# Routing sixteen tiles in groups of 4, 4, 4, 2 and 2

## What is computed

```python
x = x + L0_xattn(ctx_768, layernorm(x), mask)
x = x + L0_ffn(layernorm(x))
x = x + L1_xattn(layernorm(x), ctx_768)      # 8 heads, 77 keys
x = x + L1_ffn(layernorm(x))
...
def L1_ffn(x, router_w, w1, b1, w2, b2):
    capacity = max(1, int(Sz * 2.0 / E) + 1)                 # 257 of 1024
    scores = softmax(einsum('bsd,ed->bse', x, router_w))
    gate_vals, sel_idx = top_k(swapaxes(scores, 1, 2), capacity)
    tokens = x[b_idx, sel_idx]
    h = gelu(einsum('becd,edh->bech', tokens, w1) + b1)
    y = einsum('bech,ehd->becd', h, w2) + b2
    return zeros_like(x).at[b_idx, sel_idx].add(y * gate_vals[..., None])
```

## Time and profile before

| what | us |
|---|---|
| median of 3 runs | 962.7 (961.96 to 964.91) |
| the profiled execution | 963.34 |
| its span in the trace | 961.6 |
| mean granted clock of TensorE over the span | 0.919 of full |
| TensorE busy | 804.0 (84%) |
| VectorE, ScalarE, GpSimd busy | 552.2, 401.0, 354.6 |

### The profile page before, as it was taken

The page is one execution under the profiler, slowest core; times in us unless marked ns, Lnnn a source line. Parts: engine busy times, 40 slices in busy tenths (PEclk is TensorE's granted clock), DMA queues, the critical chain, the costliest instruction groups (busy, mean ns, idle before and its releaser), DMA issues.

```text
span 961.6 us, 12810 instructions
## 1 busy us (share of the span) xinstructions
PE 804.0 (84%) x4832; PEld 639.9 (67%) x4832; DVE 552.2 (57%) x1132; ACT 401.0 (42%) x719; POOL 354.6 (37%) x302
## 2 busy tenths in 40 slices
PE   2649988989999999988999786885139999899998
PEld 2536554755655555767789676875029988898897
DVE  5766686566666673454434477763846355655532
ACT  2324543454444334541532343332116555565563
POOL 6523112210220112243431343321443587657863
PEclk9959999999999999997999698896559999999999
DMA  6000000000000100100020201111210453245422
GB/s 174 1 0 1 1 1 1 1 1 1 1 1 0 45 3 1 44 1 3 1 84 1 88 1 45 45 45 49 93 45 6 133 138 102 47 127 137 131 30 23
DMA packets 21371, 39.70 MB, mean 41 GB/s; under 512 B 4489, under 2 KB 16893, under 8 KB 19005
## 3 DMA queue, kind: packets, MB, share of 16 engines
q1 hardware_dynamic: 14653, 30.44, 9.4%
q0 software_dynamic: 6656, 8.43, 5.0%
HBM read 30.32 MB, written 8.40 MB: 40 GB/s over the span
## 4 chain that ended last, share of the span: by engine, by line
PE 48%; DVE 20%; POOL 14%; issue 11%; ACT 5%; DMA 1%; SPq 0%; ACTq 0%; POOLq 0%; DVEq 0%
PE ps L410 14%; PE ps L549 9%; PE ps L649 5%; POOL out_dram L2351 4%; DVE mx L1152 4%; PE ps L989 4%; POOL gt L2222 3%; PE ps L513 3%; POOL wh L2346 3%; PE ps L566 2%; PE ps L567 2%; DVE qkn L1111 2%; PE ps L490 2%; POOL wh L2343 1%; DVE rep L1526 1%
## 5 line engine op out<-in xcount | busy, mean ns | idle before, releaser
L549 PE MATMUL ps<-PT,VA 128*65 128x512 f32 (+1 forms) x288 | 147.5, 594 | 0.2 <-ACT PT L1760 0.2
L989 PE MATMUL ps<-wh,he 128*128 128x256 f32 (+1 forms) x960 | 127.5, 289 | 0.0
L989 PEld LDWEIGHTS ps<-wh,he 128*128 128x128 f32 (+1 forms) x960 | 112.2, 171 | 6.7
L1760 ACT ACTIVATE PT<-ps 128x512 f32<-128x512 f32 x128 | 76.0, 594 | 67.5 <-PE ps L567 67.0
L1152 DVE TENSOR_REDUCE mx<-ps 128x1 f32<-128x1104 f32 x64 | 83.5, 1305 | 34.2 <-PE ps L513 34.0
L410 PE MATMUL ps<-GT,wh 128*128 128x258 f32 x768 | 95.5, 285 | 2.7 <-ACT het L2018 1.5
L410 PEld LDWEIGHTS ps<-GT,wh 128*128 128x128 f32 x768 | 94.2, 191 | 3.7 <-ACT het L2018 1.9
L2081 POOL TENSOR_TENSOR ssq<-ssq,half 128x4 f32<-128x4 f32 x32 | 32.4, 1013 | 127.3 <-DVE ssq L1093 127.0
L1628 DVE TENSOR_TENSOR he<-het,he 128x516 fp32r<-128x516 f32 x64 | 44.9, 702 | 59.0 <-ACT he L1654 52.5
L2072 POOL TENSOR_TENSOR rs<-rs,half 128x4 f32<-128x4 f32 (+1 forms) x18 | 17.4, 969 | 162.3 <-DVE rs L1025 162.1
L2351 POOL DMA_INDIRECT out_dram<-ye,idx x40 | 66.1, 1654 | 23.1 <-ACT ye L1654 16.0
(11 more groups left out here) (251 smaller groups left out, 1591.1 us busy)
## 6 DMA issues: line engine op xcount, KB each, us to landing
wr<-in_w1e_dram SPq DMA_DIRECT2D x8, 1024.0 KB
wr<-in_w2e_dram SPq DMA_DIRECT2D x8, 1024.0 KB
x<-in_x_dram SPq DMA_DIRECT2D x4, 512.0 KB, 7.6
w<-in_w_dram SPq DMA_DIRECT2D x2, 1024.0 KB, 4.7
y_dram<-yr SPq DMA_DIRECT2D x4, 512.0 KB, 3.0
out_dram<-x SPq DMA_DIRECT2D x4, 512.0 KB, 4.2
b2e<-in_b2e_dram SPq DMA_DIRECT2D x8, 128.0 KB
gt<-y_dram,idx POOLq DMA_INDIRECT x40
```

Source lines behind the costliest of these rows:

```text
L549: pe.matmul(bank[6 + hf][0:65, :], VA[b][0:K, kt, h, :], PT[u % 4][0:K, :], start=kt == 0, stop=kt == 8).then_inc(p_pv, 1)
L989: op = pe.matmul(bank[bk][0:M, 0:256], he[j][:, m, c0:c0 + M], w2h[i][:, 256 * m:256 * m + 256], start=n == 0, stop=n == 23)
L1760: a.activation(PT[u % 4][0:K, :], bank[4 + u % 2][0:K, :], ACT.Exp, bias=0.0 if K == 128 else mcol[:, b:b + 1]).then_inc(a_exp, 1)
```

## The change

`ROUTE` divides the router's work into five groups: tiles 0 to 3, 4 to 7, 8 to 11, 12 and 13, 14 and 15. `router` is split in two: `route_norm(r)` goes up to the normalised tiles, `route_pick(r)` takes them from the transposes to rep and scT. The statistics of a tile are now taken in `product` directly behind its addition to x, held by its semaphore. The last two groups have buffers of their own (yr2, xf2) and banks of their own (4 and 5 for the transposes, 7 and 6 for the logits). In `route_pick` they copy both halves of a tile pair in one ScalarE instruction.

```diff
+ROUTE = [(0, 4), (4, 4), (8, 4), (12, 2), (14, 2)]
...
+def last_routes(p2, n4, p3, p4):
+
+    drain(n4)
+    for stream in (p2, p2, p3, p4, p3, p3, p4, p4, p2, p3, p3, p4, p4):
+        next(stream, None)
+    drain(p2, p3, p4)
...
                 v.tensor_tensor(x[:, n, :], bank[1 + n % 2][:, 0:256], x[:, n, :], ALU.add).then_inc(v_x1, 1)
+                v.wait_ge(v_x1, n + 1)
+                step(v.bn_stats(stats[:, n, :], x[:, n, :]))
...
-            def router(g, banks, delay=0, gap=0):
-                yield from idle(delay)
-                v.wait_ge(v_x1, 4 * g + 4)
-                yield from norm(("r", g), lambda i: x[:, 4 * g + i, :], 4 * g, 4)
-                means(4 * g, ("r", g))
...
+            def route_norm(r):
+                t0, n = ROUTE[r]
+                settle()
+                for i in range(n):
+                    op = v.bn_aggr(mv[:, t0 + i, :], stats[:, t0 + i, :])
+                step(op)
+                settle()
+                v.tensor_scalar(rs[:, t0:t0 + n], mv[:, t0:t0 + n, 1], 1.0, 1e-5, ALU.mult, ALU.add).then_inc(v_var, 1)
+                yield
+                v.wait_ge(g_rstd, NORM["r", r])
+                v.scalar_tensor_tensor(nmr[:, t0:t0 + n], mv[:, t0:t0 + n, 0], -1.0, rs[:, t0:t0 + n],
+                                       ALU.mult, ALU.mult).then_inc(v_nmr, 1)
...
+                for i in range(1, n, 2):
+                    op = centred(normed_tile(r, i), x[:, t0 + i, :], t0 + i)
...
-            for g in range(1, 4):
-                qs = queries(g + 1, q_) if g < 3 else idle(0)
+            for g in range(1, 3):
+                qs = queries(g + 1, q_)
                 ns_ = norm_n(3) if g == 1 else idle(0)
-                rs_ = router(g - 1, (0,), 4, 1)
+                rs_ = both(idle(6 if g == 1 else 3), route_norm(g - 1), idle(1 if g == 1 else 4), route_pick(g - 1, 0))
                 merge(attention1(g), (qs, 0.6), (ns_, 0.8), (rs_, 1.0))
                 drain(qs, ns_, rs_)
-            drain(router(3, (0, 3)))
+            rs_ = both(idle(3), route_norm(2), idle(8), route_pick(2, 0))
+            merge(attention1(3), (rs_, 1.0), (both(idle(12), route_norm(3)), 1.0))
+            last_routes(rs_, route_norm(4), route_pick(3, 7), route_pick(4, 6))
...
-            v.wait_ge(a_scT, 2)
-            v.wait_ge(p_repT, 2)
-            v.wait_ge(d_out, 64)
+            v.wait_ge(a_scT, 3)
+            v.wait_ge(p_repT, 3)
...
+            def route_pick(r, turn, rb):
+                t0, n = ROUTE[r]
...
+                    a.wait_ge(p_rT, turns(r))
+                    copy(xf2[:, :, 256 * (r - 3):256 * (r - 3) + 256],
+                         bank[turn[0]].rearrange("p (k n) -> p k n", k=2)).then_inc(a_xf, 1)
...
+                ls = lg[:, t0:t0 + n, :]
+                a.wait_ge(v_lg, r + 1)
                 a.activation(ls, ls, ACT.Exp).then_inc(a_el, 1)
                 yield
...
+                if r >= 2:
+                    c = 128 * (t0 - 8)
+                    a.wait_ge(p_repT, r - 1)
+                    copy(scT[:, c:c + 128 * n], bank[rb][:, 0:128 * n]).then_inc(a_scT, 1)
...
+            for r, (t0, n) in enumerate(ROUTE):
+                sp.wait_ge(a_z, 4 + r + 1)
+                sp.wait_ge(v_z, 8 + r + 1)
+                src = yr[:, :, :] if r < 3 else yr2[:, 2 * (r - 3):2 * (r - 3) + 2, :]
+                sp.dma_start(yd[:, t0:t0 + n, :], src).then_inc(d_yd, 16)
+                sp.dma_start(od[:, t0:t0 + n, :], x[:, t0:t0 + n, :]).then_inc(d_out, 16)
```

213 lines of the change are left out of this document (117 added, 96 removed).

## The result

The changed kernel took 947.37 us (median of 4 runs, 944.65 to 953.81) beside 962.33 us of the kernel before (4 runs of it, 961.94 to 964.91): ratio 0.984, 95% interval 0.981 to 0.987. Two later comparisons of the same pair gave 950.04 us, 0.9843 (0.9812 to 0.9874), and 948.38 us, 0.9835 (0.9805 to 0.9866). So the change is worth about 15 us where I had forecast 7, and the time lies under the low end of my range (951.0). The sign and the places were right. The prices were not, above all those of the clock, and three of four erred to the same side.

The account below looks back on a forecast made before the run. No engine carries the whole span; the chain up to the selection's start bounds it. Terms +0.4 - 1.7 - 4.9 - 0.9 = -7.1 us take the median from 962.7 to 955.6 us; range 951.0 to 959.8, about 0.85.

Parts of the forecast that it names:

- The 3.06 us wait for yr: Group 1: TensorE's wait before the router transposes, until 619.13 us in the kernel before, was to be gone.
- the new one ahead of tile 14: Group 2: TensorE waits 3.25 us before tile 14's transposes, with half clock taken from there.
- product 15 is off the router's back: Group 2: logits and waits no longer stand between tiles 14 and 15; product 15 ends at 652.35 instead of 657.23.
- the series of three scT: Tail: three exponentials, each behind an scT, in a tail of 12 to 15 us.
- the extra round: Rival, tail: the round paid three times in series makes the tail 18.5 us, total 960.1 us; chance 0.07.
- the middle: Rival, groups 0 to 2 and tail: new waits, half clock and counted statistics eat the gain, 958.6 us; chance 0.14.
- TensorE did not stay at 1.2 GHz: Rival, from 613 us to product 15: clock stays at half, 965.6 us or above, up to 975; chance 0.04.
- the clock stays up: Rival, group 2 and tail: full clock gives 1.9 and 2.5 us more, 951.2 us; chance 0.13.
- Edit 1: Each tile's statistics directly behind its addition: one delays group 0's chain, +0.4 us, bounds 0 and +0.8.
- Edit 2: Group 1 normalised earlier: TensorE's wait for yr goes, next unit at 625.1 instead of 626.8, -1.7 us.
- Edit 3: Group 2 earlier on the vector side, TensorE's router part later: product 15 ends earlier, -4.9 us (-6.8 at full clock).
- Edit 4: Last four tiles as two groups of two: tail 14.0 us against 14.9, -0.9 us (-3.4 to +0.2).

Follow-up runs that it names:

- fours: The changed kernel with the last four tiles as one group instead of two pairs: 952.34 us, ratio 0.9863.
- stats_only: The kernel before with only each tile's statistics moved directly behind its addition, groups of four and TensorE's order as before: 962.11 us, ratio 0.9983.
- early_logits: The changed kernel with group 2's router transposes and logits early again, between the products of tiles 13 and 14, on every engine: 956.95 us, ratio 0.9932.
- warm_before: The kernel before with 30, 18, 12 and 30 dummy TensorE transposes ahead of the router transposes of groups 0 to 3: 958.52 us, ratio 0.9954.

## Why the prediction had the direction right and half the size

**What held.** The selection starts earlier by a sum of four parts; each has the sign that the walk gave it. The 3.06 us wait for yr is gone, the new one ahead of tile 14 was forecast at 3.25 us and measured 3.15, product 15 is off the router's back, the series of three scT is what ends the tail. None of the rivals that eat the gain came true: the extra round did not undo the tail (fours), the middle was not eaten, TensorE did not stay at 1.2 GHz. The rival "the clock stays up" (951.2 us, chance 0.13) came nearest, and the measured time is still 3.8 us under it; the clock did not stay up beside group 2 as it says, but came back early.

**Edit 1, +0.4: right within the noise.** +0.5 on the means, +0.8 in the pair; stats_only by itself measures as nothing. The long small VectorE instructions beside GpSimd's, which the walk took from the earlier trace rows, are there again beside group 0 (nmr 1.17 us beside a Pb of 1.23). Beside groups 1 and 2 the walk moved rs under GpSimd's Pb and nmr out from under it: nmr took 1.17 us each time before and takes 0.15 now, rs takes 0.45 and 1.04 instead of 0.17.

**Edit 2, -1.7: the term is short.** In the pair of profiles it was -2.6, on the means -3.5. The walk itself was right to 0.9 us: it set matmul rows end to end, which overlap by about 0.2 us each in the trace. The rest is on the side of before, and it is one profile of the four: tiles 6 to 10 took 26.7, 26.7, 27.1 and 30.1 us. The price of the removed wait is not what one profile shows, because the low clock behind it lasts longer in one execution than in another.

**Edit 3, -4.9: this is the step that failed most.** Measured -7.1 in the pair and -7.3 on the means. "So I take half clock from here", until product 14 at "a clock coming back": the wait came as forecast and the clock fell, but only behind the transposes of tile 14, and it was back by 638, some 3.5 us later. From those transposes to the end of product 15 the walk has 11.3 us, the trace 9.07. Product 13 was priced right (3.4 us at half clock, measured 3.25). Of the 2.2 us half is clock taken as low that was not: transposes of tile 14 0.74 us instead of 1.35, of tile 15 1.06 instead of 1.2, product 14 2.04 instead of 2.2, the router's transposes 1.04 instead of 1.3. The other half is no clock at all: each row starts 0.16 to 0.25 us before the one ahead of it ends, 1.1 us over the six, and the walk set them end to end. The stretch that I took for low is as long as the two in the earlier trace rows, over 6 us each, and I had put the other value (-6.8, the clock stays up) aside for a rival. Between them I chose by the nearest wait (3.06), and a wait of that length says that the clock falls, not for how long it stays down. early_logits shows where the gain comes from: with group 2's turn early, the whole 8 us of this segment is gone again.

**Edit 4, -0.9: mis-sized in the same way.** Measured -2.8 in the pair, two terms that cover the missing 1.9: GpSimd's power on 2 columns takes 0.70 us instead of the 1.01 that I chose as the upper bound (0.3), and the clock held until 5.5 us behind the start of the last addition, so the logits took 2.18 us in all instead of 3.55 and the transposes ahead of them 0.66 instead of 1.0 (1.7). I had worked out -3.4 for full clock throughout, and called full clock to 6 the less likely end, because before the change the clock fell 2.1 us behind the last product. But there TensorE had nothing to do behind it; now it has group 2's logits and tiles 12 and 13's transposes, the work that the change moved there. I had moved the work in my walk, and kept the clock of the idle place.

**The rest.** -11.6 us in the pair of profiles, -13.0 on the means; the medians say -15. About 2 us lie outside the stage: 1.5 us at the start of tile 0's addition, where the program is the same and 20 profiles range over 10.6 us, and 0.9 behind cnd. No run shows that the change causes them, and none shows what does. The first comparison was also the luckiest of three for the changed kernel: 947.37 us, then 950.04 and 948.38.

**How much is clock.** Filling the waits in the kernel before is worth 4.4 us of the 15 (warm_before), and beside group 1 it gives in the profile what Edit 2 gives, so that the gain of Edit 2 can be read as the clock's. (No run undoes Edit 2 alone; its size rests on the profiles.) The early place of group 2's turn costs about 8 us, and 4.5 with its waits filled. So about a third of the 15 us can be had by the clock alone. The other 10 are the shorter chain and clock that dummies did not save (beside group 2 warm_before did not hold it); these runs don't part the two.

**The range.** It was built from the ends of single terms, each taken near its dear end. Clock stays up in group 2 (-1.9) and in the tail (-2.5) were added only in one rival, and group 1 had no upside at all. With what the pair of profiles shows for all four terms (-11.6 instead of -7.1) my own sum would have been 962.7 - 11.6 = 951.1, just the low end of the range. The last 3.7 us, down to 947.4, are in no term of mine. Against them stand 1.4 us in the stage of before (109.9 in my profile, 111.3 on the mean of four) and the 1.5 and 0.9 outside the stage, whose cause is open.

## What to carry to other kernels

- Where an order takes a wait out of TensorE's way, price both what the wait costs and the low clock behind it, and take the latter from several profiles: with the same 3.06 us wait in it one step took 9.6 to 13.0 us. Where only one profile is there, keep both clocks as the two ends of every term.
- Walk matmul rows with their overlap: six rows set end to end were 1.1 us too long here.
- When work is moved into a place, its clock must be walked anew with that work in it. TensorE work that waits for no one (logits of a group long normalised) is best kept for the place where TensorE would otherwise run dry.
- A gain of 3 to 4 us that two profiles agree on can be missing from the medians. Under 0.5% a profile says where to look, not what it is worth.
